# Layer 2 of a fused two-layer graph attention kernel: where VectorE's five low parts per group read their probabilities from

## The reference

```python
Wh = x @ W
e = leaky_relu((Wh @ a1)[:, None] + (Wh @ a2)[None, :], 0.2)
att = softmax(where(adj > 0, e, -9e15), axis=1)
h = elu(att @ Wh)
out = layernorm(x + h)
```

## Time and profile before

| | us |
|---|---|
| median of 3 runs | 1436.32 (1435.98 to 1436.86) |
| the profiled execution, its own time | 1435.78 |
| its span, from the first to the last instruction | 1434.0 |
| layer 2 in it (from 970 to the end) | 464 |
| one full group of layer 2 (1131.6 to 1206.2) | 74.6 |
| TensorE busy in that group | 74.26 |
| VectorE, ScalarE, GpSimd busy in that group | 70.42, 47.54, 70.46 |

### The profile page before, as it was taken

One profiled execution on the slowest core, in us unless ns is written; L12 is line 12 of the kernel. 1 busy time (PEld: TensorE's weight loads), 2 busy tenths in 40 slices (PEclk: granted clock), 3 DMA queues, 4 the chain that ended last, 5 costly groups with the idle time before them and its releaser, 6 DMA issues.

```text
span 1434.0 us, 28674 instructions
## 1 busy us (share of the span) xinstructions
PE 1408.5 (98%) x9745; PEld 1017.8 (71%) x9745; DVE 1295.9 (90%) x2176; ACT 1108.6 (77%) x2483; POOL 1193.4 (83%) x895
## 2 busy tenths in 40 slices
PE   8999999999999999999999999999999999999997
PEld 4677777777777777777777777786666666676764
DVE  6999999999999999999899999969999999999997
ACT  6788888888888888888888888878757666656565
POOL 6888888888888888888888878857989989898985
PEclk9999999999999999999999999999999999999998
DMA  8999999999999999999999999855534434443520
GB/s 269 299 270 276 256 264 255 271 268 274 269 259 257 257 272 276 274 266 260 258 259 275 271 273 254 225 119 109 106 71 103 89 82 90 101 88 86 107 59 16
DMA packets 427953, 291.42 MB, mean 203 GB/s; under 512 B 356896, under 2 KB 403232, under 8 KB 427808
## 3 DMA queue, kind: packets, MB, share of 16 engines
q1 hardware_dynamic: 427808, 289.59, 74.6%
HBM read 160.56 MB, written 40.89 MB: 140 GB/s over the span
## 4 chain that ended last, share of the span: by engine, by line
PE 91%; DVE 3%; POOL 3%; ACT 2%; issue 1%; DMA 0%; POOLq 0%; DVEq 0%; SPq 0%; ACTq 0%
PE ps L684 17%; PE ps L713 11%; PE ps L769 11%; PE ps L779 10%; PE ps L686 9%; PE ps L724 8%; PE ps L726 8%; PE ps L725 8%; PE ps L750 6%; POOL p_lo L587 2%; DVE rows L1112 1%; PE ps L651 1%; PE ps L793 1%; POOL rstd L597 1%; DVE neg_mask L1077 1%
## 5 line engine op out<-in xcount | busy, mean ns | idle before, releaser
L924 ACT ACTIVATE rows<-rows,exp_bias 128x512 f32<-128x512 f32 x576 | 417.4, 725 | 55.9 <-DVE exp_bias L1087 55.8
L587 POOL TENSOR_TENSOR p_lo<-p,p_hi 128x1024 fp32r<-128x1024 f32 x171 | 403.4, 2398 | 31.3 <-ACT p_hi L972 24.1
L1112 DVE CUSTOM_DVE_ANT_0 rows<-ps,neg_mask 128x1024 f32<-128x1024 f32 x288 | 352.3, 1223 | 79.5 <-PE ps L726 72.0
L495 POOL TENSOR_SCALAR edges<-neg_mask 128x1536 uint8<-128x1536 bf16 x190 | 307.3, 1618 | 95.7 <-DVE neg_mask L1077 83.8
L1206 DVE SCALAR_TENSOR_TENSOR p<-ps,e_col,edgesT 128x1024 f32<-128x1024 f32 x288 | 349.7, 1278 | 7.9 <-PE ps L743 7.4
L684 PE MATMUL ps<-vals,pT_hi 128*128 128x256 f16 x1536 | 294.6, 273 | 0.2
L910 ACT CAST pT_hi<-ps 128x512 f16<-128x512 f32 x384 | 223.3, 581 | 89.6 <-PE ps L713 89.5
L537 POOL TENSOR_TENSOR inp_sb<-rows,inp_sb 128x512 f16<-128x512 f32 x192 | 281.7, 1487 | 8.2 <-DVE inp_sb L1121 0.7
L972 ACT CAST p_hi<-p 128x1024 fp32r<-128x1024 f32 x196 | 199.7, 1047 | 108.2 <-DVE p L1206 102.7
L686 PE MATMUL ps<-vals,pT_lo 128*128 128x128 f16 x1536 | 274.1, 219 | 0.0
L1128 DVE TENSOR_TENSOR pT_lo<-ps,pT_hi 128x512 f16<-128x512 f32 x384 | 250.8, 684 | 3.7 <-ACT pT_hi L910 3.7
(11 more groups left out here) (129 smaller groups left out, 1960.6 us busy)
## 6 DMA issues: line engine op xcount, KB each, us to landing
adj_sb<-adj SPq DMA_DIRECT2D x192, 768.0 KB, 5.6
edge_rows<-edges SPq DMA_DIRECT2D x192, 192.0 KB, 4.8
xq<-x SPq DMA_DIRECT2D x48, 64.0 KB, 3.0
xr<-x SPq DMA_DIRECT2D x48, 64.0 KB, 5.8
out<-y_w SPq DMA_DIRECT2D x5, 512.0 KB, 3.5
inp_sb<-inp SPq DMA_DIRECT2D x3, 768.0 KB, 8.2
inp_sb<-inp_sb SPq DMA_TRANSPOSE x96, 4.6
edgesT<-edge_rows SPq DMA_TRANSPOSE x48, 5.4
```

The lines of the kernel that those rows point to most:

```text
L587: nc.gpsimd.tensor_tensor(p1_lo[:, m % LO_SLOTS, :], p1[:, (NB * g + n) % P_SLOTS, :], p1_hi[:, m % HI_SLOTS, :].bitcast(F32), ALU.subtrac ...
L924: nc.scalar.activation(row_chunk(1 - par, c), row_chunk(1 - par, c), ACT.Exp, bias=exp_bias[:, 1 - par:2 - par], scale=EXP_SCALE, accum_ou ...
L1112: nc.vector.tensor_tensor_reduce(row_pair(par, k), scores_pair(k), neg_mask_row[:, 2 * k * CHUNK:2 * (k + 1) * CHUNK], 1.0, -3.0e38, ALU.a ...
```

## The change

The copy of the probabilities to PSUM (`copy_rows`), its semaphore and the PSUM view go. VectorE's low parts take `p1` from its slot in SBUF, so both of their inputs are in SBUF. They wait for the high part of the block and for a free low slot, as before. ScalarE's exponential of `elu_parts` no longer waits for VectorE's low parts, which had shared its PSUM banks.

```diff
-        p1_ps = ps[:, EX0:EX0 + 2, :].rearrange("p b w -> p (b w)")
...
-            def copy_rows(g, n):
-                act.wait_ge(p1_set, NB * g + n + 1)
-                after(act, dve_lo_set, dves_until(g, n))
-                act.wait_ge(v_set, g)
-                nc.scalar.copy(p1_ps, p1[:, (NB * g + n) % P_SLOTS, :]).then_inc(p1_copied, 1)
...
                 after(act, v_set, w if q < NG - 1 else NG - 1)
-                after(act, dve_lo_set, dves_until(q + 1, 0))
...
-                    if g < NG and by_dve(g, n):
-                        copy_rows(g, n)
                     if g < NG and (split_in(g, n) or by_dve(g, n)):
                         high_part(g, n)
...
             def low_rows(g, n):
                 m = highs_until(g, n)
-                dve.wait_ge(p1_copied, dves_until(g, n) + 1)
                 dve.wait_ge(hi_set, m + 1)
                 after(dve, lo_used, m + 1 - LO_SLOTS)
-                nc.vector.tensor_tensor(p1_lo[:, m % LO_SLOTS, :], p1_ps, p1_hi[:, m % HI_SLOTS, :].bitcast(F32),
+                nc.vector.tensor_tensor(p1_lo[:, m % LO_SLOTS, :], p1[:, (NB * g + n) % P_SLOTS, :], p1_hi[:, m % HI_SLOTS, :].bitcast(F32),
                                         ALU.subtract).then_inc(dve_lo_set, 1)
```

More of the change, by code:

```diff
@@ L298, in build @@
         hi_set, hi_used, lo_set, lo_used = sem("hi_set"), sem("hi_used"), sem("lo_set"), sem("lo_used")
-        p1_copied, dve_lo_set = sem("p1_copied"), sem("dve_lo_set")
+        dve_lo_set = sem("dve_lo_set")
         late_hi_set, late_lo_set = sem("late_hi_set"), sem("late_lo_set")
```

## The result

The changed kernel takes 1450.73 us (median of 5 runs, 1450.56 to 1450.80), against 1436.32 us before. The ratio is 1.0099, with a 95% interval of 1.0087 to 1.0112: 14.4 us slower. The forecast was 1452.3.

What follows compares the result with a forecast made beforehand. TensorE was taken as the bound, with VectorE and GpSimd right behind. A loss of 3.3 us in each of groups 1 to 4 (13.2) and 2.85 in the last made 16.0 us, giving 1452.3 us, range 1442 to 1461.

Steps and rivals of the forecast that it cites:

- What bounds: Full group of layer 2: TensorE bounds, busy 74.26 of 74.60 us; 4 us more on VectorE or GpSimd makes a new bound.
- The copies are worth nothing: ScalarE's 25 copies of 1.01 us and its waits of 4.8 us in five groups: removal valued at nearly nothing.
- The subtraction itself: VectorE's low part with both inputs in SBUF: left alone, it stays at 1.22 us.
- VectorE waits for GpSimd: VectorE's SBUF subtraction is held until GpSimd's running instruction ends, then gets in ahead of the next one.
- GpSimd waits for VectorE: GpSimd's next low part is held while VectorE's subtraction runs: 1.0 us each, bounds 0 and 1.1.
- The schedule behind block 31: Blocks 33, 38 and 43 each delay GpSimd 1.0 us; less a margin of 0.2, 2.8 us per group, groups 1 to 4.
- Block 25 at nothing, block 28 at 0.5 in each group: Ahead of block 31: block 25's low part costs nothing; block 28's meets GpSimd's power, 0 to 1.0 us, taken as 0.5.
- The last group: GpSimd has 8 low parts behind block 31 and a margin of 0.65: 3.0 - 0.65 + 0.5 = 2.85 us lost.
- (a): Rival: only VectorE is held; TensorE waits at the row terms, 3.2 us in each of four groups: 1449 us; chance 0.14.
- (b): Rival: VectorE and GpSimd both bound, block 28's chain takes all; about 5 us a group, 25 in all: 1461; chance 0.12.
- (c): Rival: no contention at full width, or it finds gaps; TensorE stays the bound, copies were free: 1436 us; chance 0.10.
- (d): Rival: faster, as ScalarE's relief removes TensorE's stall at block 31, at most 6 us: 1430 us; chance 0.04.

## Why the prediction was right

**What bounds.** Right. TensorE was busy for all but 0.3 us of a full group, GpSimd and VectorE were next, and the first edit that cost them 3 us in a group made a new bound.

**The copies are worth nothing.** Right, shown alone: 0.9998. The credit of 1.0 us to VectorE at block 33 was real too: its wait for the high part there fell from 1.50 to 0.44 us.

**The subtraction itself.** Right. Block 28's, which nothing held, took 1.21 us with both inputs in SBUF.

**VectorE waits for GpSimd.** Right. The five 128-column rows of group 0 were enough to see it, and the full-size ones end 1.08 us after GpSimd's instruction, where 1.09 was worked out.

**GpSimd waits for VectorE.** Right, 0.96 us each where 1.0 was taken. The lower bound of 0 that the 128-column rows had left open is excluded. The Trainium skill, "SBUF — State Buffer", section "Who interferes with whom", states the contention for VectorE instructions with two SBUF inputs; the block for a whole instruction it spells out for VectorE's two-port modes, and the prediction took it over for this form. The trace agrees for the low parts, with 3.38 us instead of 2.4, and so does the kernel with two halves; GpSimd's short power did not block.

**The schedule behind block 31.** The forecast had 2.8 us in groups 1 to 4; a full group shows 2.9. With three holds of 0.96 and a margin of 0.2 it should have been 2.7, so the margin was mis-sized. The third pair behind 1196.44 starts at 1197.45 in the trace, not at the 1197.56 that I worked out, and GpSimd's block 47 ends at 1197.39, so TensorE starts 0.06 us behind it. In the changed kernel the two stand at 1204.13 and 1204.19: 0.06 again. So before the change there was no margin left at all, and a row of the waits of weight loads in the full group from 1131.6, which I had not read, says so: TensorE's load for this pair already waited for GpSimd. Before, and now:

```profile
PEld ps L750 <- POOL p_lo L587: 0.4, 1, 0.4
```

```profile
PEld ps L749 <- POOL p_lo L586: 3.8, 4, 1.0
```

**Block 25 at nothing, block 28 at 0.5 in each group.** The mechanism was priced in the wrong place. Block 28's subtraction got in at once in the middle of GpSimd's power (1169.52, 1.21 us), and the chain to block 31 moved by less than 0.1. Block 25's is free only where GpSimd waits for a slot, which I had read in one full group and carried over to group 1. There it lengthened the stall at block 31 by 1.1 us, and the lower clock came behind it. In the sum: 13.2 us forecast for groups 1 to 4, 4.0 + 8.9 = 12.9 measured, the parts differently spread. That the sum comes so near is in part luck: the margin and the blocks 25 and 28 were each off, group 1 was lost to a longer stall, the lower clock and VectorE and not to GpSimd's low parts, and the differences cancel.

**The last group.** 2.85 forecast, 2.1 measured. Block 28's 0.5 was not there, 0.1 came ahead of block 31, and behind it GpSimd's eight low parts take 21.80 us instead of 18.88, of which 2.0 reach the output product (25.09 us from block 31's first product, against 23.07). So the margin there was 0.9 us, where 0.65 was taken.

**The rivals.** (a) is no fiction: with GpSimd left alone, or given room, VectorE's lateness makes a group of 75.5 us, between TensorE's 74.6 and the 77.6 measured, and with the copies kept it is VectorE that TensorE's products wait for. I had priced it at 3.2 us in a group, where 0.9 is measured in these two kernels: in a full group of the changed kernel VectorE's waits for GpSimd at blocks 33, 38 and 43 were 0.4 to 0.9 us each and not 2.2. (b) did not occur in the full groups; in group 1, VectorE's longest low part took 3.3 us, 2.1 of them waiting, and TensorE stood 1.4 us at the turn for it. (c) and (d) are excluded.

## What to carry to other kernels

Before an operand of a VectorE instruction is moved from PSUM to SBUF, look whether GpSimd is busy beside it: here a subtraction with two SBUF inputs and GpSimd's low parts excluded each other for whole instructions, so both got slower, and the PSUM copy on an engine with time to spare was the price of keeping them apart. Look for a small instruction of the same form in the trace: one was enough to see that VectorE is held, though not what GpSimd loses. The cost is then the hold less the margin of the late engine at that place, read from its restart to the last thing that waits for it, weight loads included, in the first group as well as in a repeated one.

## What the runs showed of the hardware that was not expected

GpSimd's power on 8 columns, 1.67 us long, did not hold VectorE's subtraction (1.21 us in the middle of it), while its full-size low parts did for as long as they ran. Two short instructions of VectorE in a row cost more than one long one, 4.41 us against 1.78, since GpSimd's came between them; in the last group, where GpSimd had finished, block 43's two halves took 1.28 us together. Stalls of TensorE of 1.88 to 1.97 us were followed by a granted clock of 0.79 over 8 us in three kernels (the changed one, the one with the copies kept and the one with blocks 25 and 28 alone), where one of 0.83 us at the same place was followed by 1.00.
